# Rotary halves exchanged by SBUF transfers instead of projected twice, in a graph, attention and expert layer

## What is computed

```python
h = _rmsnorm(x, ln1_w)
q = (h @ wq.T).reshape(Bx, Tx, NH, HD).transpose(0, 2, 1, 3)      # NH 4, HD 32
k = (h @ wk.T).reshape(Bx, Tx, NKV, HD).transpose(0, 2, 1, 3)     # NKV 2
q = q * cos + _rotate_half(q) * sin       # _rotate_half: [-upper 16, lower 16] of each head's 32
k = k * cos + _rotate_half(k) * sin
```

## Time and profile before

| | |
|---|---|
| median of 3 runs | 3580.86 us (3577.54 to 3583.05) |
| profiled execution | 3581.53 us, span 3579.8 us |
| mean granted TensorE clock | 0.937 |
| graph stage, second pass | about 890 to 1333 us of the span |
| 16 strips' projections and rotations | first rotate 914.36, last 1317.24 us |
| TensorE busy from 1200 to 1300 us | 98.05 of 100 us |

### The profile page before, as it was taken

How to read it: one execution, slowest core, us unless ns; L and a number is a source line. 1 busy time by engine, 2 the same in 40 slices (tenths; PEclk the granted TensorE clock), 3 DMA queues, 4 the chain that set the end, 5 groups by cost and what they waited for, 6 DMA issues and landing times. The chain is left out here.

```text
span 3579.8 us, 56821 instructions
## 1 busy us (share of the span) xinstructions
PE 3099.7 (87%) x22369; PEld 1361.4 (38%) x22369; DVE 2571.3 (72%) x2752; ACT 1424.0 (40%) x2843; POOL 1684.5 (47%) x1082
## 2 busy tenths in 40 slices
PE   2678889899899969999999999999999999829990
PEld 1334434344444433433333333333333333315650
DVE  8888886764554537779778877778877888227774
ACT  0000000000000004656666666666766666726660
POOL 0000000000212214666887689777789778734664
PEclk9778999999999978999999999999999999969995
DMA  9898875777768834522220000000000000012226
GB/s 379 337 385 360 360 311 241 311 300 260 269 259 328 327 131 159 209 88 85 100 70 10 10 24 18 7 13 7 11 18 18 1 12 9 13 66 59 72 66 238
DMA packets 170430, 531.94 MB, mean 149 GB/s; under 512 B 20721, under 2 KB 66938, under 8 KB 125254
## 3 DMA queue, kind: packets, MB, share of 16 engines
q1 hardware_dynamic: 124328, 473.74, 34.3%
q10 hardware_dynamic: 33024, 31.47, 2.6%
q0 software_dynamic: 12816, 23.11, 2.0%
HBM read 434.70 MB, written 92.15 MB: 147 GB/s over the span
## 5 line engine op out<-in xcount | busy, mean ns | idle before, releaser
L1231 DVE TENSOR_REDUCE unit_max<-ps_max 128x2 f32<-128x1024 f32 (+2 forms) x1088 | 1226.0, 1171 | 309.3 <-PE ps_max L1460 265.0
L1007 POOL TENSOR_TENSOR chunk_sum<-chunk_sum,probs 128x1024 f32<-128x1024 f32 x480 | 1132.1, 2359 | 309.0 <-ACT probs L1101 299.1
L1101 ACT ACTIVATE probs<-ps_ring 128x512 f32<-128x512 f32 x2112 | 1089.8, 596 | 437.3 <-PE ps_ring L1479 404.2
L566 PE MATMUL ps_gather<-ring,keep_attended 128*128 128x512 f32 x1688 | 791.6, 626 | 140.4 <-DMA ring<-in_adj 121.7
L1479 PE MATMUL ps_ring<-q_stack,keep_shared 97*128 97x512 f16 x2112 | 674.6, 385 | 28.3 <-ACT probs L1101 22.8
L1494 PE MATMUL ps_acc<-probs,keep_shared 128*32 128x256 f32 (+1 forms) x8448 | 565.3, 386 | 0.0
L566 PEld LDWEIGHTS ps_gather<-ring,keep_attended 128*128 128x128 f32 x1688 | 333.3, 202 | 542.7 <-issue 542.7
L367 DVE TENSOR_TENSOR work<-work,ring 128x2048 f32<-128x2048 f32 x195 | 446.6, 2290 | 36.0 <-DMA ring<-in_adj 32.4
L342 POOL DMA_DIRECT2D scratch_lower<-lower x13 | 7.3, 559 | 807.7 <-ACT lower L484 807.7
L1460 PE MATMUL ps_max<-k_heads,q_heads 32*128 32x512 f16 (+3 forms) x2176 | 275.6, 378 | 68.9 <-DVE unit_max L1231 47.4
L1503 PE MATMUL ps_acc<-probs,keep_ones_heads 128*32 128x256 f32 (+1 forms) x4224 | 327.3, 379 | 0.0
(11 more groups left out here) (244 smaller groups left out, 2669.2 us busy)
## 6 DMA issues: line engine op xcount, KB each, us to landing
ring<-in_adj SPq DMA_DIRECT2D x302, 1024.0 KB, 14.1
keep_shared<-in_adj SPq DMA_DIRECT2D x45, 1024.0 KB, 11.1
scratch_slots<-empty_rows SPq DMA_DIRECT2D x16, 2080.0 KB, 14.1
scratch_parts<-empty_part SPq DMA_DIRECT2D x8, 2048.0 KB, 13.3
moe_parts<-scratch_parts SPq DMA_DIRECT2D x64, 256.0 KB, 4.4
moe_x_rows<-scratch_slots SPq DMA_DIRECT2D x39, 260.0 KB, 2.7
x_in<-in_x SPq DMA_DIRECT2D x16, 256.0 KB, 13.4
x_in<-in_x ACTq DMA_DIRECT2D x16, 256.0 KB, 8.0
```

The source lines that it names most:

```text
L566: last = nc.tensor.matmul(bank[:], support[:, s * SUB + c, :], tile_of[g, is_again][:, c * BT:(c + 1) * BT], start=(first and c == 0), sto ...
L1007: steps.then(nc.gpsimd.tensor_tensor(totals, totals, weights, ALU.add))
L1101: nc.scalar.activation(probs[:, q % SLOTS, i, kv, :, lo:], halves(bank)[:, :, lo:], ACT.Exp, scale=SCALE).then_inc(ring_read, 1)
L1231: nc.vector.tensor_reduce(unit_max[:, half % 2, heads, s % 2, unit], ps_max[:, base:base + HEADS, at:at + width], AX_X, ALU.max).then_inc( ...
```

## The change

The two projections with exchanged weights and their weights go. `rotate` now multiplies q and k in PSUM by sin (into `crossed`) and by cos (into `rotated`). ACT then issues eight transfers per strip from SBUF to SBUF (`swap_halves`), each of 16 partitions by 4 KB, that write `crossed` with its halves exchanged into `swapped`. A new piece on DVE, `split`, due one step after `rotate`, adds `swapped` to `rotated` and rounds to fp16. The stores of strip n are issued by ACT one strip later, behind the eight transfers and the tables of the strip after it.

```diff
     due += [(begins[n], 2, n) for n in range(NB)] + [(begins[n] + 5, 1, n) for n in range(NB)]
+    due += [(begins[n] + 6, 3, n) for n in range(NB)]
...
-        rope_a, rope_b = work[:, 2], work[:, 3]
+        crossed = work[:, 2:4]
...
-        ps_q, ps_q_half, ps_k, ps_k_half = ps_support, ps_gather[2], ps_gather[3], ps_degrees
+        ps_q, ps_k = ps_support, ps_gather[3]
...
             def rotate(n):
                 if n:
+                    dve.wait_ge(split_ready, 2 * n)
+                dve.wait_ge(tables_loaded, n * 32 + 32)
+                dve.wait_ge(qk_ready, n + 1)
+                for m, plain in enumerate((ps_q, ps_k)):
+                    nc.vector.tensor_tensor(crossed[:, m], plain[:], sin, ALU.mult).then_inc(crossed_ready, 1)
+                    nc.vector.tensor_tensor(rotated[m][:], plain[:], cos, ALU.mult).then_inc(crossed_ready, 1)
+
+            def split(n):
+                if n:
                     dve.wait_ge(split_stored, n * 48)
...
-                dve.wait_ge(tables_loaded, n * 32 + 32)
-                dve.wait_ge(qk_ready, n + 1)
-                for m, (plain, half, hi) in enumerate(((ps_q, ps_q_half, q_hi), (ps_k, ps_k_half, k_hi))):
-                    nc.vector.tensor_tensor(rope_a, plain[:], cos, ALU.mult)
-                    steps.then(nc.vector.tensor_tensor(rope_b, half[:], sin, ALU.mult))
-                    steps.then(nc.vector.tensor_tensor(rotated[m][:], rope_a, rope_b, ALU.add))
+                dve.wait_ge(crossed_ready, 4 * n + 4)
+                dve.wait_ge(swapped_in, SWAPS * (n + 1))
+                for m, hi in enumerate((q_hi, k_hi)):
+                    steps.then(nc.vector.tensor_tensor(rotated[m][:], rotated[m][:], swapped[:, m], ALU.add))
                     steps.then(nc.vector.tensor_copy(hi[:], rotated[m][:]))
                 dve.sem_inc(high_ready, 1)
...
+            def swap_halves(n):
+                act.wait_ge(crossed_ready, 4 * n + 4)
+                for row in range(0, NH * HD, HD):
+                    for to, src in ((row, row + HD // 2), (row + HD // 2, row)):
+                        act.dma_start(swapped[to:to + HD // 2], crossed[src:src + HD // 2]).then_inc(swapped_in, 16)
+
+            def store_split(n):
+                act.wait_ge(split_ready, 2 * n + 2)
+                cols = slice(finished[n] * BT, (finished[n] + 1) * BT)
+                for name, tile in (("q_hi", q_hi), ("q_lo", q_lo), ("k_hi", k_hi)):
+                    act.dma_start(dram[name][:, cols], tile[:]).then_inc(split_stored, 16)
...
-                act.wait_ge(high_ready, n + 1)
+                swap_halves(n)
                 if n + 1 < NB:
                     load_tables(n + 1)
-                act.wait_ge(split_ready, 2 * n + 2)
...
+                if n:
+                    store_split(n - 1)
+            store_split(NB - 1)
...
             def project(n):
                 pe.wait_ge(h_copied, n + 1)
                 if n:
-                    pe.wait_ge(high_ready, n)
+                    pe.wait_ge(crossed_ready, 4 * n)
                     pe.wait_ge(v_copied, n)
...
-                for out, w in ((ps_q, wq), (ps_q_half, wq_half), (ps_k, wk), (ps_k_half, wk_half)):
+                for out, w in ((ps_q, wq), (ps_k, wk)):
                     last = nc.tensor.matmul(out[:], w[:], hT, start=True, stop=True)
```

More of the change, by code:

```diff
@@ L159, in graph_stage @@
         x1, z = by_subtile(work[:, 0]), by_subtile(work[:, 1])
-        rope_a, rope_b = work[:, 2], work[:, 3]
+        crossed = work[:, 2:4]
         cos, sin, hT = work[:, 4], work[:, 5], work[:, 6]
         rotated = [sb(f"rotated{n}", [P, BT]) for n in range(2)]
-        reduced = [sb(f"reduced{n}", [P, BT]) for n in range(2)]
+        swapped = sb("swapped", [P, 2, BT])
+        reduced = [swapped[:, n] for n in range(2)]
         inv_sqrt_degree = sb("inv_sqrt_degree", [P, NB * SUB])
@@ L178, in graph_stage @@
         wT = sb("wT", [C, C])
-        wq, wq_half = sb("wq", [C, C]), sb("wq_half", [C, C])
-        wk, wk_half = sb("wk", [C, C]), sb("wk_half", [C, C])
+        wq, wk = sb("wq", [C, C]), sb("wk", [C, C])
         wv = sb("wv", [C, NKV * HD])
@@ L232, in graph_stage @@
         z_ready = sem("z_ready")
+        crossed_ready = sem("crossed_ready")
+        swapped_in = sem("swapped_in")
         high_ready = sem("high_ready")
@@ L266, in graph_stage @@
         STACKED_BY_POOL = NB - 2
+        SWAPS = 2 * NH * 16
         def stack_keys(queue, n, stacked):
@@ L292, in load_x @@
                 sp.dma_start(x_in[:], x_dram[t]).then_inc(x_loaded, 16)
-            for w, d in ((wT, "wT"), (wq, "wq"), (wq_half, "wq_half"), (wk, "wk"), (wk_half, "wk_half"),
-                         (wv, "wv"), (ln1, "ln1")):
+            for w, d in ((wT, "wT"), (wq, "wq"), (wk, "wk"), (wv, "wv"), (ln1, "ln1")):
                 sp.dma_start(w[:], dram[d]).then_inc(weights_loaded, 16)
@@ L462, in _ @@
             for _, kind, n in sorted(due):
-                (gather_strip, rotate, normalize)[kind](n)
+                (gather_strip, rotate, normalize, split)[kind](n)
         @block.scalar
         def _(act):
-            act.wait_ge(weights_loaded, 16 * 7)
+            act.wait_ge(weights_loaded, 16 * 5)
             def root_degrees(t):
@@ L547, in turn @@
                 last.then_inc(signal, 1)
-            pe.wait_ge(weights_loaded, 16 * 7)
+            pe.wait_ge(weights_loaded, 16 * 5)
             pe.wait_ge(constants_ready, 9)
@@ L2011, in rotary_tables @@
     emb = np.concatenate([freqs, freqs], axis=-1)
-    sign = np.where(np.arange(HD) < HD // 2, -1.0, 1.0).astype(np.float32)
+    sign = np.where(np.arange(HD) < HD // 2, 1.0, -1.0).astype(np.float32)
     cos, sin = np.cos(emb), np.sin(emb) * sign
@@ L2026, in laid_out @@
     adj = a["adj"].reshape(NB, BT, NB, SUB, P).transpose(0, 2, 4, 3, 1).reshape(NB, NB, P, SUB * BT)
-    half = np.concatenate([np.arange(HD // 2, HD), np.arange(HD // 2)])
     q_rows = np.arange(NH * HD).reshape(NH, HD)
@@ L2035, in laid_out @@
         "x": a["x"], "adj": adj, "wT": a["gnn_W"].T,
-        "wq": wq[q_rows.ravel()].T, "wq_half": wq[q_rows[:, half].ravel()].T,
-        "wk": wk[k_rows.ravel()].T, "wk_half": wk[k_rows[:, half].ravel()].T,
+        "wq": wq[q_rows.ravel()].T, "wk": wk[k_rows.ravel()].T,
         "wv": a["ffn_wv"].T, "wo": a["ffn_wo"].T, "ln1": a["ffn_ln1_w"][:, None], "ln2": a["ffn_ln2_w"][:, None],
```

## The result

The changed kernel takes 3644.44 us (median of 4 runs, 3641.73 to 3650.07) against 3579.32 (4 runs, 3577.54 to 3583.05): the ratio is 1.0183, 95% interval [1.0165, 1.02]. It is 65 us slower. The forecast was 3607 and its range ended at 3630, so the sign was right and the size was not.

The account below looks back on a forecast made before the run. The prediction took TensorE to bound the second pass, with ACT's transfers sometimes last. Terms of +2 (up to 1132), +19.4 (two rounds) and +5.1 (the end) gave +26.5 us: 3607 us, range 3573 to 3630.

Parts of the forecast that it names:

- What goes: Two of four projections per strip on TensorE: 1.72 us saved for each of fifteen strips, 3.4 for strip 15.
- Up to 1132: Second pass until SP's load at 1132.58, strips 0 to 8: savings and longer chains sum to +2 us, bounds -12.5 and +9.
- The square roots wait less than a microsecond more: Sign expected in the profile after: ACT's square roots wait less than 1 us more than before.
- Issues of 0.45 us: ACT's swaps, tables and stores: 0.45 us per issue, 5.9 us per strip; 8.3 at 0.64 each.
- From a rotation to the gather: Strips 8, 10, 12: gather ends 14.2 us after the projection without a burst; TensorE waits at least 3.0 us.
- The gather's idle time ends on a swap or a store landing: Sign expected on DVE: the gather's idle time ends on a landing of a swap or store, not on TensorE.
- The two rounds: SP's rounds from 1132 and 1188: 67.6 and 62.5 us long instead of 55.3 and 55.4, so +12.3 and +7.1 us.
- The lower ends of the rounds: Earliest split starts in the two rounds, 43 and 39.3 us into them; together given as +10.9 us.
- the second rival: Savings and delays in the second pass cancel: +3.5 us, 3584 us, within 8 us of either side; chance 0.12.
- The end: From 1243 on: strip 15's normalization +6.8 us, last rotation to POOL's end +7.6, less savings; sum +5.1.
- The third: Issues cost 0.64 us or more in five chains, or swaps push stores late: +42 us, 3623 us; chance 0.14.
- three signs of being wrong: Rounds staying near 55 us, stores landing within 3 us in bursts, or swaps landing over 15 us after issue everywhere.

Follow-up runs that it names:

- e4: Kernel before without the two exchanged projections, plain ones used in their place, nothing else changed: 3577.76 us, ratio 0.9987.
- e1: Changed kernel without its eight transfers per strip, the split adding the unexchanged product: 3579.18 us, ratio 0.9991.
- e5: Kernel before with eight transfers of 16 partitions by 4 KB per strip added to ACT's queue, read by nothing on the path: 3635.03 us, ratio 1.0148.
- e6: Changed kernel with all its transfers, but the split neither waits for them nor adds their result: 3647.39 us, ratio 1.0175.
- e7: Changed kernel with ACT issuing the stores of x1 and z behind the second square root and the copy of hT: 3646.45 us, ratio 1.018.
- e2: Changed kernel with the eight transfers per strip issued by POOL instead of ACT: 3624.94 us, ratio 1.0129.
- e12: Kernel before with eight transfers of 16 partitions by 128 B per strip added to ACT's queue: 3606.78 us, ratio 1.0082.
- e11: Kernel before with one transfer of 128 partitions by 4 KB per strip added to ACT's queue: 3595.91 us, ratio 1.0043.
- e13: Kernel before with four copies on ACT per strip, 4.28 us in all, and no added transfer: 3591.12 us, ratio 1.003.

## Why the forecast had the sign and missed the size

- **What goes (29.2 us).** The size was right: the projections fell by 28.4 us. It failed as a saving. "Work taken off it is worth its own time wherever nothing else ends later" was read from TensorE's best stretch. e4 shows what it is worth: 4 us, 10 at most. The pass was already bound in turns by TensorE and ACT's landings, which the earlier trace rows showed, and I voided only some 4 us for it.
- **Up to 1132 (+2, bounds -12.5 and +9).** This is the step that failed most. SP's load at 1132.58 now comes at 1159.28, +26.7 us. I priced four places at which a longer chain lies (three landings of k_hi, strip 8's gather) and let the other strips save. There was no term for the load that eight transfers put on ACT and its queue in every strip. The same load of SP comes at 1126.64 in e1, which has the new order without the transfers, at 1155.46 in e5, which has the transfers in the old order, and at 1158.97 in e6, whose split doesn't wait for them. So the new order with the missing projections alone was worth -5.9 us up to here, and the transfers cost 32.6 on top of it, 22.9 in the old order.

```profile
1126.64 0.33 SPq L312 DMA_DIRECT2D lower<-scratch_lower  x1
```

```profile
1155.46 0.33 SPq L311 DMA_DIRECT2D lower<-scratch_lower  x1
```

- **"The square roots wait less than a microsecond more."** Wrong, by 45.8 us over the pass for the second one and 15.4 for the first. I took an issue to cost 0.45 us whatever stands in the queue. In the changed order this wait could be exchanged for another (e7); in the old order (e5) it is the wait that the load raised most, by 34.5 us.
- **Issues of 0.45 us.** They took 0.61 (median of 128), near the upper bound of 0.64. That is 1.7 us more for a strip's thirteen issues: 933.91 to 941.48 is 7.6 us, and 5.9 were taken.
- **From a rotation to the gather (14.2 us after the projection).** Right in kind, as the two timelines below show, of DVE at strip 10 and of TensorE at the four turns that wait for a gather. From the start of the rotation to the end of the gather it is 16.1 us, and 1.7 of the difference are the issues. TensorE waits 4.6 to 7.6 us there, where I had 3.0 as the least; the 14 us at the last two (strips 11 and 13) were too much (7.57 and 6.18).

```profile
1214.71 0.69 DVE L455 TENSOR_TENSOR work<-ps_support,work 128x512 f32<-128x512 f32 x1 [2.44 <-POOL k_lo L354]
...
1227.56 0.69 DVE L468 TENSOR_TENSOR rotated<-rotated,swapped 128x512 f32<-128x512 f32 x1 [10.36 <-DMA scratch_k_hi<-k_hi]
...
1230.14 0.69 DVE L413 TENSOR_TENSOR work<-ps_gather,lower 128x512 f32<-128x512 f32 x1 [0.24 <-DVE k_hi L469]
```

```profile
1114.93 1.11 PE L566 MATMUL ps_turn<-keep_ident,transposed 128*128 128x128 f32 x4 [4.60 <-DVE transposed L413]
...
1159.31 1.11 PE L566 MATMUL ps_turn<-keep_ident,work 128*128 128x128 f32 x4 [4.79 <-DVE work L413]
...
1230.89 1.11 PE L566 MATMUL ps_turn<-keep_ident,work 128*128 128x128 f32 x4 [7.57 <-DVE work L413]
...
1298.50 1.12 PE L566 MATMUL ps_turn<-keep_ident,work 128*128 128x128 f32 x4 [6.18 <-DVE work L413]
```

- **"The gather's idle time ends on a swap or a store landing."** Right: on the store of k_hi, issued behind the swaps. The swaps' own landing doesn't decide there: in e6, which doesn't wait for it, the waits are the same.
- **The two rounds (+12.3, +7.1).** Mechanism right, size short: +16.2 and +12.2. SP's loads, which mark the rounds, after:

```profile
1159.28 0.33 SPq L312 DMA_DIRECT2D lower<-scratch_lower  x1
...
1230.86 0.33 SPq L312 DMA_DIRECT2D lower<-scratch_lower  x1
...
1298.47 0.33 SPq L312 DMA_DIRECT2D lower<-scratch_lower  x1
```

Rounds of 71.6 and 67.6 us, where I had 67.6 and 62.5. Splits 9 and 11, for whose start I had 48.5 and 43.4 us into the round, and 50.3 and 46.3 at the latest, start at 50.7 and 47.2:

```profile
1209.93 0.69 DVE L468 TENSOR_TENSOR rotated<-rotated,swapped 128x512 f32<-128x512 f32 x1 [5.74 <-DMA scratch_k_hi<-k_hi]
...
1278.07 0.69 DVE L468 TENSOR_TENSOR rotated<-rotated,swapped 128x512 f32<-128x512 f32 x1 [4.17 <-DMA scratch_k_hi<-k_hi]
```

These later landings are 6.0 of the 9.1 us that were missing in the two rounds. The chain behind each, 19.1 us forecast, took 20.9 and 20.4, which the dearer issues (1.7 us) about explain. The lower ends of the rounds were also added up wrongly: 43 + 19.1 - 55.3 and 39.3 + 19.1 - 55.4 make +9.8 and not +10.9, which moves the second rival by 1 us.

- **The end (+5.1).** +11.6 measured. The last rotation to the end of POOL took 15.4 us (1376.06 to 1391.48), forecast 15.0. What was missing lies ahead of it: TensorE waited 19.22 us for strip 15's normalization, which stands on DVE behind split 14 and its landing (8.80 at the same place before).
- **Rivals.** The third was nearest. Its cause, dearer issues and swaps that push the stores, is a part of what the runs found (ACT's late square roots are the other), but I priced it in five chains (3623), not in every strip. The rule against many small transfers (the Trainium skill, "DMA: Bandwidth & Descriptors", "Rules for kernel authors") points the right way: the same bytes cost 15.7 us in one transfer and 53.3 in eight. The way in which I let it act, about 2 us each in series, did not occur: the eight are issued 0.63 us apart in the strip shown, and the 128 of the pass land 2.4 us (median; 10.6 at most) after their issue.
- **The queue.** The Trainium skill, same page, "Issuing engines are not separate DMA queues", says that issuing from several engines only saves the time of the issue, usually small beside the transfer. Here the other queue gave back 19 us (e2), and DVE's wait for the second square root fell from 53.4 to 25.9 with it; how much of that is ACT's time and how much the order in its queue, no run separates. What the prediction took from the Trainium skill, same page, "Anatomy of one DMA", is a fit given there for transfers that POOL issues; the stores here are ACT's, and between 1.9 and 23.0 us no one figure fits them.

In sum the terms were +2, +19.4 and +5.1 and came out at +26.7, +28.4 and +11.6. The sign was no luck, since the rounds and the end were right in kind. The size failed through two errors on one side: the saving was worth a seventh of what I put in, and the load on ACT and its queue in every strip had no term. None of the three signs of being wrong appeared: the rounds grew, stores in a burst landed late (23.0 us), and the swaps landed within 10.6 us.

## What to carry to other kernels

Price a new transfer by what is queued behind it in every strip, not only in the chains that wait for it. Three variants tell the two apart: one without the transfers (e1), one that issues them without using their result (e6), and the kernel before with the transfers added (e5). When a queue already ends some waits, work taken from another engine is worth what is left after those waits have grown. Leaving that work out, before its replacement is built, gives the ceiling (e4: 4 us of 28.4). And a wait that vanishes while the time stays has moved: in e7 from the square root to the next landing in the same queue.

## What the runs showed of the hardware

- An issue on ACT can be held far beyond its usual length: x1's store took 0.33 to 0.34 us at 16 of 16 places before, and up to 7.34 us after, and the square root that stands behind it came 9.00 us late. The hold varies with count and bytes (9.3 us for the pair of issues in e5, 7.0 in e12, 4.9 in e11), but 4.2 us came in e13 without any transfer more.
- A transfer of 16 partitions by 4 KB between SBUF buffers takes 0.61 us (median) to issue on ACT; the stores of 128 KB beside it 0.44 to 0.45.
- Landing times in ACT's queue follow the burst: the same 128 KB of k_hi landed 23.0 us after issue at 941 us, and 1.9 us after issue at 1385.
- TensorE's waits cost twice: with 114.3 us idle in place of 39.5, the mean granted clock over the pass went from 0.96 to 0.88 (full is 2.4 GHz, the lower level 1.2), and the same 704 matmul records on the ring took 18.6 us more.
